# One-hots ahead of the masks, table products a step sooner, and both state halves together on the tensor engine

## The reference

```python
q = x @ Wq; k = x @ Wk; v = x @ Wv          # 16 heads of 16 channels
local_out  = _local_attn(lq, lk, lv)        # 4 heads, windows of 128 tokens looking one window back
global_out = _causal_linear_attn(gq, gk, gv)# 12 heads
# linear: q = softmax(q), k = elu(k) + 1, blocks of 64 tokens (u)
bk_cumsum = jnp.cumsum(bk.sum(axis=-2), axis=-2)
ctx = jnp.cumsum(jnp.einsum('bhund,bhune->bhude', bk, bv), axis=2)
ctx = ctx / (bk_cumsum[..., None] + 1e-06)  # then shifted by one block
attn = jnp.einsum('bhund,bhude->bhune', bq, ctx)
# experts: top 2 of 8 by xf @ router_w.T, softmax of the two scores as weights
out += gelu(xf @ w1[e].T) @ w2[e].T * w_e   # hidden 1024, for each of 8 experts
```

## Time and profile before

| | us |
|---|---|
| three runs | 806.52, 802.04, 806.2 |
| median | 806.2 |
| the profiled execution | 804.93 |
| its span, first to last instruction | 803.2 |

### The profile page before, as it was taken

How to read it: one execution, slowest core, us unless ns; L and a number is a source line. 1 busy time by engine, 2 the same in 40 slices (tenths; PEclk the granted TensorE clock), 3 DMA queues, 4 the chain that set the end, 5 groups by cost and what they waited for, 6 DMA issues and landing times.

```text
span 803.2 us, 21487 instructions
## 1 busy us (share of the span) xinstructions
PE 706.1 (88%) x6866; PEld 555.4 (69%) x6867; DVE 459.0 (57%) x1540; ACT 405.9 (51%) x1115; POOL 429.5 (53%) x423
## 2 busy tenths in 40 slices
PE   1899999975887878898689999999999999999883
PEld 1666666743554545566478888888888888888662
DVE  6788887779978887865533333433444333334331
ACT  4788888733554545676344333444443444334331
POOL 6777777635444444477224555555655554543522
PEclk9999999969889887999699999999999999999998
DMA  8354333221131212132124444444444444433421
GB/s 255 119 158 134 120 107 107 93 66 47 49 84 51 70 43 72 46 114 57 50 53 67 78 77 75 77 79 78 77 77 74 77 79 73 72 64 57 61 44 20
DMA packets 87991, 64.26 MB, mean 80 GB/s; under 512 B 54675, under 2 KB 81556, under 8 KB 87924
## 3 DMA queue, kind: packets, MB, share of 16 engines
q1 hardware_dynamic: 73204, 43.69, 20.0%
q0 software_dynamic: 13632, 18.91, 15.5%
q10 hardware_dynamic: 1088, 0.79, 0.3%
HBM read 36.08 MB, written 17.96 MB: 67 GB/s over the span
## 4 chain that ended last, share of the span: by engine, by line
SPq 38%; PE 27%; DVE 15%; issue 9%; DMA 4%; ACT 4%; POOL 2%; DVEq 0%; POOLq 0%
SPq L688 37%; PE bank L279 9%; DVE ss L1303 4%; PE bank L1107 3%; DVE spare L505 3%; PE bank L1125 2%; PE bank L1066 2%; PE bank L1177 2%; DMA out<-attn,rows_to 2%; ACT ss L951 2%; PE bank L1128 1%; DMA out<-res,rows_to 1%; DVE xin L506 1%; PE bank L1086 1%; PE bank L1131 1%
## 5 line engine op out<-in xcount | busy, mean ns | idle before, releaser
L279 PE MATMUL bank<-stage,w1h 128*128 128x256 f16 (+1 forms) x1248 | 198.7, 267 | 6.1 <-DMA stage<-xin 4.7
L279 PE MATMUL bank<-stage,w1l 128*128 128x256 f16 (+1 forms) x624 | 164.9, 266 | 0.0
L1215 PE MATMUL bank<-w2h,pt 128*128 x568 | 154.9, 273 | 5.3 <-issue 4.0
L1215 PE MATMUL bank<-w2l,pt 128*128 x568 | 154.8, 273 | 0.0
L1215 PE MATMUL bank<-w2h,spare 128*128 x568 | 154.8, 273 | 0.0
L279 PEld LDWEIGHTS bank<-stage,w1h 128*128 x1248 | 115.9, 99 | 25.9 <-issue 8.9
L1026 ACT ACTIVATE pt<-ss 128x512 f16<-128x512 f32 (+1 forms) x78 | 41.9, 585 | 164.6 <-PE bank L1215 141.7
L876 POOL DMA_INDIRECT out<-res,rows_to x36 | 63.7, 1770 | 73.8 <-DMA stage<-rows 53.1
L876 POOL DMA_INDIRECT out<-attn,rows_to x35 | 61.9, 1769 | 73.4 <-DMA out<-attn,rows_to 47.7
L1477 DVE TENSOR_SCALAR res<-bank,tables 128x256 f32<-128x256 f32 x36 | 17.4, 484 | 96.3 <-PE bank L1215 78.6
L951 ACT ACTIVATE ss<-ss,negmax 128x256 f32<-128x256 f32 x128 | 63.8, 500 | 16.1 <-DVE negmax L1303 15.8
(11 more groups left out here) (242 smaller groups left out, 1661.8 us busy)
## 6 DMA issues: line engine op xcount, KB each, us to landing
stage<-w1c SPq DMA_DIRECT2D x16, 512.0 KB, 3.4
stage<-w2c SPq DMA_DIRECT2D x16, 512.0 KB
w1h<-x SPq DMA_DIRECT2D x16, 256.0 KB, 3.8
xn_rows<-w2h SPq DMA_DIRECT2D x32, 128.0 KB, 2.8
xb<-x SPq DMA_DIRECT2D x32, 128.0 KB, 2.8
out<-res SPq DMA_DIRECT2D x32, 128.0 KB, 2.0
stage<-xin SPq DMA_TRANSPOSE x144
stage<-rows SPq DMA_TRANSPOSE x140
```

Source lines behind the costliest of these rows:

```text
L279: ins = pe.matmul(dst, lhs(a, k), rhs(c, k), start=(n == 0), stop=(n == len(terms) - 1))
L1215: ins = pe.matmul(bY[h][:, 0:D], (hh, hl)[a][:, f, h * P:(h + 1) * P], (w2h, w2l)[c][:, DS(which * (FC * D) + f * D, D)], start=(f == a == ...
```

## The change

It makes five edits.

1. **One-hots.** DVE makes all six columns of a batch ahead of the masks: three right behind lrow, ahead of the wait for the output projection (`pr_ps`), three at the place of the former first half. The second place, behind the state sums, is empty.
2. **Table products** run on PE one step after their one-hots (before: two), the table sums likewise, and `TABLE` falls by one, and with it the step of POOL's first gathers and of the slot tables.
3. **State halves.** PE makes both halves at one place, behind the transposes of q: half 0 into bank 5, half 1 into the upper part of bank 2, from partitions 0 to 63 and 64 to 127. DVE adds both, one behind the other. The transposes of q go to bank 5. `raw` holds two tiles (four halves), its first halves are set ahead of the steps.
4. **Waits.** The value projection waits for the second sum (`state2_in`) where it waited for `qgt_in`; POOL's mask waits for `lin_ps` of the tile before.
5. **Single buffers**: `krelu`, `state` and `qgt` have one buffer each where they had two.

```diff
-        qs, krelu, ke = pair("qs", [P, D]), pair("krelu", [P, GD]), pair("ke", [P, D])
+        qs, krelu, ke = pair("qs", [P, D]), 2 * [sb("krelu", [P, GD])], pair("ke", [P, D])
-        state = pair("state", [P, 2, CTX])
-        raw = pair("raw", [P, 2, CTX])
+        state = 2 * [sb("state", [P, 2, CTX])]
+        raw = pair("raw", [P, 4, CTX])
-        qgt = pair("qgt", [P, 2, P])
+        qgt = 2 * [sb("qgt", [P, 2, P])]
...
-        b_qgt = b_tok1[:, D:2 * D]
+        b_qgt = b_ctx[:, 0:D]
-        TABLE = HOT + 1 + BATCHES
+        TABLE = HOT + BATCHES
...
 # POOL
-                        t.wait(s["lin_ps"], -3)
+                        t.wait(s["lin_ps"], -2)
...
 # ACT
-                        t.wait(s["ctx1_ps"], min(-2, NT - 3 - t.t))
+                        t.wait(s["ctx_ps"], -2)
-                        t.wait(s["ke_in"], -2)
+                        t.wait(s["ke_in"], -1)
...
 # PE
-                        if t.has(0):
-                            t.wait(s["state0_in"], 0)
-                        add_to_state(t, 0)
+                        t.wait(s["state2_in"], -2)
+                        v = val[b][t.odd(-1)]
+                        parts = [(slice(0, 64), b_ctx[:, D:D + CTX]), (slice(64, P), b_tok1[:, D:D + CTX])]
+                        for r, dst in parts:
+                            pe.matmul(dst[:, 0:CB], ke[b][r, 0:GA], v[r, VL:VL + CB], start=True, stop=True)
+                        for r, dst in parts:
+                            ins = pe.matmul(dst[:, CB:CTX], ke[b][r, GA:2 * GA], v[r, VL + CB:VC],
+                                            start=True, stop=True)
+                        ins.then_inc(s["ctx_ps"], 1)
...
-                    if t.has(-1) and t.has(1):
-                        t.wait(s["state1_in"], -1)
-                        add_to_state(t, 1)
...
-                        t.wait(s["qgt_in"], -1)
+                        t.wait(s["state2_in"], -1)
...
 # DVE
-                            dve.tensor_tensor(raw[b][:, 0, :], b_state[:, b * CTX:(b + 1) * CTX], raw[b][:, 1, :], ALU.add)\
-                               .then_inc(s["state0_in"], 1)
+                    if HOT <= t.t < HOT + BATCHES:
+                        route_onehots(dve, t.t - HOT, 0, 3)
...
-                        if HOT + 1 < t.t <= TABLE:
-                            route_sum(dve, t.t - HOT - 2)
+                        if HOT < t.t <= TABLE:
+                            route_sum(dve, t.t - HOT - 1)
...
                     if HOT <= t.t < HOT + BATCHES:
-                        route_onehots(dve, t.t - HOT, 0, 3)
+                        route_onehots(dve, t.t - HOT, 3, CH)
...
-                        t.wait(s["ctx0_ps"], -1)
-                        dve.tensor_tensor(raw[b][:, 1, :], b_state[:, b * CTX:(b + 1) * CTX], raw[b][:, 0, :], ALU.add)\
+                        t.wait(s["ctx_ps"], -1)
+                        dve.tensor_tensor(raw[b][:, n + 1, :], b_ctx[:, D:D + CTX], raw[b][:, n, :], ALU.add)\
                            .then_inc(s["state1_in"], 1)
                         t.wait(s["state1_in"], -1)
+                        t.wait(s["mask_in"], -3)
+                        dve.tensor_tensor(raw[b][:, (n + 2) % 4, :], b_tok1[:, D:D + CTX], raw[b][:, n + 1, :], ALU.add)\
+                           .then_inc(s["state2_in"], 1)
...
-                    if HOT <= t.t < HOT + BATCHES:
-                        route_onehots(dve, t.t - HOT, 3, CH)
```

More of the change, by code:

```diff
@@ L169, in block_kernel @@
                  "v_in kneg_in kexp_in qmax_in qsub_in qexp_in tok0_read qsum_in qrec_in ke_in qgt_ps "
-                 "head0 head1 head2 head3 negmax0 negmax1 prob0 prob1 pt_ps pta_in ptb_in ctx0_ps ctx1_ps state0_in state1_in mask_in "
+                 "head0 head1 head2 head3 negmax0 negmax1 prob0 prob1 pt_ps pta_in ptb_in ctx_ps state1_in state2_in mask_in "
                  "lin_ps lrow_in rden_in qgt_in att_ps rrec_in latt_in ath_in atl_in loch_in locl_in pr_ps res_in "
@@ L176, in block_kernel @@
         rows_stored = [sem(f"rows_stored{n}") for n in range(SLOTS)]
-        raw_zero = sem("raw_zero")
+        raw_zero, begun = sem("raw_zero"), sem("begun")
         res_stored = [sem(f"res_stored{b}") for b in range(2)]
@@ L285, in halves_of @@
             return lambda a, k: xt[:, a * D + k * P:a * D + (k + 1) * P]
-        b_xnt, b_tok0, b_tok1, b_s, b_state, b_att, b_out = bank[0], bank[1], bank[2], bank[3:5], bank[5], bank[6], bank[7]
-        b_qgt = b_tok1[:, D:2 * D]
+        b_xnt, b_tok0, b_tok1, b_s, b_ctx, b_att, b_out = bank[0], bank[1], bank[2], bank[3:5], bank[5], bank[6], bank[7]
+        b_qgt = b_ctx[:, 0:D]
         TE = NT * E
@@ L1069, in scores_of @@
                                     ins.then_inc(s[f"head{h}"], 1)
-                def add_to_state(t, u):
-                    b, v, r = t.row(-1), val[t.row(-1)][t.odd(-1)], slice(u * 64, u * 64 + 64)
-                    dst = b_state[:, b * CTX:(b + 1) * CTX]
-                    pe.matmul(dst[:, 0:CB], ke[b][r, 0:GA], v[r, VL:VL + CB], start=True, stop=True)
-                    pe.matmul(dst[:, CB:CTX], ke[b][r, GA:2 * GA], v[r, VL + CB:VC], start=True, stop=True)\
-                        .then_inc(s[f"ctx{u}_ps"], 1)
                 def step(t):
@@ L1225, in _ @@
                 pe.wait_ge(s["stage_lo"], NT)
-                for n in ("tok0_read", "qsub_in", "v_in", "state1_in", "pta_in", "ptb_in", "qgt_in", "atl_in",
+                for n in ("tok0_read", "qsub_in", "v_in", "state1_in", "state2_in", "pta_in", "ptb_in", "qgt_in", "atl_in",
                           "latt_in"):
@@ L1286, in _ @@
                         dve.memset(val[b][odd][:, VC - 1:VC], 1.0)
+                dve.wait_ge(raw_zero, 2)
+                for b in range(2):
+                    dve.memset(raw[b][:, 0, 0:CTX:CTX - 1], 1e-6).then_inc(begun, 1)
                 dve.wait_ge(pool_const, CONSTANTS)
```

21 lines of the change are left out of this document (9 added, 12 removed).

## The result

The changed kernel takes 765.4 us (median of 4 runs, 763.8 to 766.6) where the kernel before takes 805.0 on the same chip (4 runs, 802.0 to 806.5): a ratio of 0.951, 95% interval 0.948 to 0.955. Its profiled execution took 764.7 us, span 762.9 (before 804.9 and 803.2). The forecast was 768, from 767 for a profiled execution.

What follows compares the result with a forecast made beforehand. It saw hot steps bound by PE waiting for DVE's qgt, queued behind one-hots held by POOL. Gains 30 (hot) + 0.7 (step 27 to 28) + 6 (early) + 1 (late) = 37.7 us gave 768 us; range 757 to 786.

Steps and rivals of the forecast that it cites:

- qgt's wait goes, DVE is next: Hot steps: PE's 27.3 us of waits for qgt vanish, DVE becomes late next; period 13.29 to 10.3, 30 us gained.
- Four held one-hots: Hot steps: the first four one-hots come out singly at the ends of four POOL instructions, the fourth at M+8.15.
- the 0.2 for hand-overs: Hot period: 0.2 us added for hand-overs to the summed M+10.1, giving 10.3.
- x, the price of the second half beside the first: PE's state matmuls: added cost of making both halves together, between 0 and 0.58 us, taken as 0.25.
- Early steps: Early attention steps: PE gains 0.6 each, taken as 0.5 over 12 periods, 6 us, bounds 0 and 8.
- The second sum covered in early steps: DVE's second state sum, 0.35 us, moved earlier: costs nothing since POOL holds the scaling anyway; uncovered, 3.5 us.
- Routing steps 14 to 16: DVE sets the pace; the moved second sum removes as much behind lrow as it adds: nothing, at worst 1 us.
- Single buffers, table a step sooner: Single krelu, state and qgt have slack, and table products and sums move whole to a step earlier: nothing for either.
- No hold: Rival, hot steps: one-hots slip between POOL's instructions or POOL has finished; period 9.2, 757 us; chance 0.08.
- The slow clock: Rival, hot steps: PE falls cold, or the hold works against POOL; period 11.5 to 12, 779 to 785 us; chance 0.17.
- The new wait: Rival: state2_in behind mask_in, or single qgt, makes each step wait and eats most gain; around 797 us; chance 0.05.
- The slower rival: Rival, hot steps: each first-batch instruction may wait for its own POOL instruction; period from 14, about 815 us; chance 0.04.

Runs made afterwards that it cites:

- e1_onehots: Kernel before with only the one-hots all ahead of the masks and the table products and gathers a step sooner; 773.8 us, ratio 0.962.
- e5_act: Changed kernel with POOL's scaling of the staged weights given to ACT in the eleven hot steps; 756.5 us, ratio 0.941 to the kernel before.
- e7_order: e5_act with POOL's low-weights subtraction moved earlier and its bias addition moved to the step's end in hot steps; 748.2 us, ratio 0.932 to the kernel before.
- e3_serial: Changed kernel with the state's second half computed from the same array rows as the first (result wrong); 768.7 us, ratio 0.956 to the kernel before.
- e8_early: e7_order with POOL's scaling of staged weights put behind the masked state and atl in steps before the hot ones; 744.4 us, ratio 0.927 to the kernel before.
- e11_apart: Changed kernel with the state's second half made at its old place, behind the products of q and k, in its own bank; 812.9 us, ratio 1.011 to before.
- e9_warm: Changed kernel with 24 needless PE products in each of the three steps behind the routing work; 760.7 us, ratio 0.948 to the kernel before.
- e12_fill: e8_early with 29, 24 and 29 needless PE products in the three steps behind the routing work; 736.8 us, ratio 0.917 to the kernel before.
- e6_single: Kernel before with only krelu, state and qgt as single buffers, POOL's and ACT's waits one step nearer; 804.2 us, ratio 1.002.
- e2_states: Changed kernel with the one-hots and table products put back to their old places; 786.2 us, ratio 0.979 to the kernel before.
- e10_best: e8_early with 24 needless PE products in each of the three steps behind the routing work; 743.4 us, ratio 0.924 to the kernel before.

## Why the prediction was right, and where it was off

- **qgt's wait goes, DVE is next: right.** The line is gone, qgt stands at 231.64 (M+2.90), lrow at M+4.88 (forecast "near M+5.4"). e1_onehots shows that the order of the one-hots does it, not the bank.
- **Four held one-hots: right, instruction by instruction.** The forecast had them come out at the ends of L843, L815, L821 and L828 (L844, L815, L821 and L828 now), the fourth at M+8.15; it came out at M+8.14. The pair, the table sum with res, and the three pairs then take 0.37, 0.47 and 1.11 as forecast, but they start at 236.78 (M+8.04), 0.10 before the fourth's record ends: the forecast added to an end what it had read from start to start, and came to 10.1. The mis-sized term is the 0.2 for hand-overs; it was 0. So 10.00, not 10.3. That the hold sets the period is shown by e5_act and e7_order, which change only what POOL does beside the one-hots. That the stretch came out near the forecast (-31.4 for -30) is in part luck: the first of the ten periods gained nothing, and the others gained more than 3.0.
- **x, the price of the second half beside the first: 0, taken 0.25.** The eight instructions take 0.59 where four took 0.58. By the Trainium skill, TensorEngine Tiling (Array Packing), section "Theoretical Speedup", two tiles of 64 rows may reach twice the speed; the trace agrees, and e3_serial prices the other case at 0.45. In late steps the term was mis-sized and miscounted: the forecast had 0.3 in each of four periods, and the halves gave 0.57 in the one ordinary period that had a second half to save. That the four came to 1.0 together, as forecast, is luck.
- **Early steps: size right (0.5 a step taken, 0.53 measured over the thirteen), reason half right.** The gain was put down to PE's 0.58, less something for an engine close behind, thought to be ACT. The engine close behind is DVE with POOL: e8_early shortens DVE's held scalings, PE's wait at L1080 goes and the period falls to 8.90. e3_serial does not decide it, since its 0.45 falls into the wait for ACT, as the forecast said of x. That PE set the period before the change was not tested. e11_apart shows what the togetherness needs: DVE must get both sums ahead of POOL's long instruction.
- **The second sum covered in early steps: right**, and by a cover that can be missed: 1.74 us later it is POOL's 2.13 us that holds the scalings.
- **Routing steps 14 to 16 "nothing, at worst 1": +1.7 in the two profiles.** This step of the forecast looked only at DVE's work and left out PE's clock. Behind its second wait for lrow PE came out at the full clock before (2.25 us idle, then L1125 0.65 for sixteen), and at 1.2 GHz in the changed kernel (4.82 idle, then L1119 1.08); DVE stands 2.00 for PE ahead of M16 in place of 0.66. e9_warm and e12_fill show that the clock is the price there. That the change is what lets the clock fall is not shown: in e6_single, which has the order and the halves of the kernel before, PE comes out of that wait (1.94) at 1.2 GHz too and the three steps take 48.4, while e1_onehots has 46.7.
- **Single buffers, table a step sooner: nothing, right** for the buffers (e6_single); the table was never run by itself. Its product and sum moved 0.12 from one late period to the one before.
- **The rivals.** No hold (757) did not come. Its price was mis-sized: the forecast let PE decide at 9.2 without the hold, but e7_order, with one one-hot held, has 8.20. The slow clock came in the first hot period alone (0.75; 0.97 over the ten). The new wait of PE at L1080 is at most 0.4 long between M3 and M13. The expert stage, 377.7 of 397.0 us busy, is as before. The slower rival's mechanism, a POOL instruction for each one-hot, is what happened, to four of the first batch's six and not at full length.

## What to carry to other kernels

When two engines hold each other off, write down both timelines and compare the ends: here each held DVE one-hot ended 0.05 us after a POOL instruction, and moving POOL's work beside DVE's masks and sums (e7_order) gave 7 to 8 us without changing a sum. A wait has a queue behind it: take away the late producer (e1_onehots, -32) before the bank that it blocks (e2_states, -20). And where an engine stands long for another in a few steps, look at its clock behind the wait: the kernel that keeps PE busy with needless products through three waits is 7.6 us faster than the one without (e12_fill against e8_early, on two chips). In the two profiles, 7.4 apart, the three routing periods hold 3.7 of it and the first hot period 1.4; the rest lies in stretches where the two kernels do the same.

## What was not expected of the hardware

- In the hot steps POOL was not delayed by the queued one-hots: its four instructions stand back to back within 0.05 us (L844 ends at 234.51, L815 starts at 234.47), yet one DVE instruction gets through at each joint. By the Trainium skill, SBUF — State Buffer, section "Who interferes with whom", when DVE runs in a two-port mode, whoever issues first holds the shared ports for the whole instruction and the other blocks; the trace agrees for DVE. POOL is seen longer elsewhere: its L821 takes 1.17 in place of 0.72 in a routing step (190.11), where it starts beside DVE's L492 (189.74 to 190.70, both inputs in SBUF), and the same pair is in the kernel before (195.42, 1.17).
- In the hot and the early steps only DVE's tensor_scalar instructions out of SBUF (one-hots, scalings) were seen held. Between 232.4 and 234.5, with POOL's L844 running, qt and kt (0.28), qsum (0.34), the reciprocals and lrow (0.42) have the lengths that they have elsewhere. In a routing step a scan out of SBUF was held as well: L470 (128x8) takes 0.95 beside POOL's L828 and ends 0.02 behind it (172.85, 172.74 and 1.04), where the kernel before, with no POOL instruction beside it, has 0.17.
- With needless products in the waits, 1.27 us of idle time behind them was followed by 1.2 GHz from the second row on, 1.38 (third wait, e10_best) within the first row, and 1.50 (third wait, e9_warm) after 1.6 us at the full clock; 0.81 in e9_warm's first was not. Without such products 1.94 idle (e6_single) was followed by 1.2 GHz, and 2.25 in the same place of the kernel before was not. The length of the gap alone does not decide, and these cases give no rule.
- The same order of DVE's sums is worth -20 us with PE's halves together (e2_states) and, together with all the rest of the change, +7 us with them apart (e11_apart).
